# Expert units' down products: from f32 to three f16 high/low products, with the split on ScalarE and GpSimd

## What is computed

```python
def _L0_ffn_ref(hidden_states, router_w, e_bias, Wg, Wu, Wd, SWg, SWu, SWd):
    x = hidden_states.reshape(-1, orig_shape[-1])            # 2048 tokens, 128 features
    topk_idx, topk_w = _route(x, router_w, e_bias)           # 8 of 64 experts
    coef = zeros((T, E)).at[arange(T)[:, None], topk_idx].add(topk_w)
    g = einsum('th,ehi->tei', x, Wg)                         # 64 experts, 64 inner features each
    u = einsum('th,ehi->tei', x, Wu)
    h = silu(g) * u * coef[:, :, None]
    moe_out = einsum('tei,eih->th', h, Wd)
    shared = silu(x @ SWg) * (x @ SWu) @ SWd
    return (moe_out + shared).reshape(orig_shape)
```

## Time and profile before

| | |
|---|---|
| median of 3 executions | 1024.77 us (1020.2 to 1024.84) |
| span of the profiled execution | 1022.1 us (its own time isn't reported apart from the span; the span lies between the times of the three executions) |
| recurrence begins / units begin | about 43 us / 166 us |
| recurrence ends / last unit's down product | 514 us / 608 us |
| transformer block | 608 to 1022 us |
| TensorE, VectorE, GpSimd, ScalarE busy | 89%, 72%, 55%, 47% |

### The profile page before, as it was taken

How to read it: one execution, slowest core, us unless ns; L and a number is a source line. 1 busy time by engine, 2 the same in 40 slices (tenths; PEclk the granted TensorE clock), 3 DMA queues, 4 the chain that set the end, 5 groups by cost and what they waited for, 6 DMA issues and landing times. The chain is left out here.

```text
span 1022.1 us, 32080 instructions
## 1 busy us (share of the span) xinstructions
PE 910.5 (89%) x13472; PEld 719.5 (70%) x13472; DVE 737.8 (72%) x1834; ACT 479.4 (47%) x899; POOL 566.1 (55%) x516
## 2 busy tenths in 40 slices
PE   3498659999999999999998988999999999998886
PEld 3376547778777877778776866777777777777554
DVE  5766685876777676676779655878878778777655
ACT  2234323333232322223232216778787778877752
POOL 3688832343343433334354554766776766767663
PEclk9655556999999999999999997999999999999998
DMA  9212007442222222223233420000000000000001
GB/s 251 47 26 59 20 19 148 107 100 83 67 64 82 69 78 72 63 64 85 65 88 102 126 63 2 3 3 3 3 3 4 3 3 3 3 3 3 3 1 42
DMA packets 46532, 51.81 MB, mean 51 GB/s; under 512 B 22165, under 2 KB 37302, under 8 KB 46390
## 3 DMA queue, kind: packets, MB, share of 16 engines
q1 hardware_dynamic: 43472, 48.78, 18.6%
q10 hardware_dynamic: 2918, 1.01, 0.6%
HBM read 48.20 MB, written 1.57 MB: 49 GB/s over the span
## 5 line engine op out<-in xcount | busy, mean ns | idle before, releaser
L763 POOL TENSOR_TENSOR ex<-ex,xn 128x512 f32<-128x512 f32 x128 | 163.9, 1281 | 248.9 <-ACT thcb L1016 160.2
L1016 ACT ACTIVATE thcb<-ps 128x512 f32<-128x512 f32 x132 | 78.9, 598 | 205.5 <-PE ps L1874 199.5
L849 POOL TENSOR_TENSOR wu<-encC,wu 128x1024 f16<-128x1024 f32 x64 | 135.6, 2134 | 27.5 <-ACT encC L1094 27.3
L1889 PE MATMUL ps<-ex,wd 128*128 128x256 f32 x512 | 140.3, 396 | 1.3 <-POOL ex L763 0.9
L1440 DVE SCALAR_TENSOR_TENSOR ex<-thcb,ps 128x512 f32<-128x512 f32 x132 | 90.5, 686 | 50.0 <-ACT thcb L1016 45.5
L1874 PE MATMUL ps<-xnT,wg 128*128 128x256 f16 x768 | 107.1, 276 | 1.5 <-DVE ex L1446 1.4
L843 POOL TENSOR_TENSOR wd<-wd,a_sum 128x512 f32<-128x512 f32 x64 | 66.7, 1043 | 72.8 <-DVE a_sum L1571 72.6
L1874 PE MATMUL ps<-xnT,wu 128*128 128x256 f16 x768 | 106.8, 276 | 0.0
L1943 PE MATMUL ps<-wg,M 128*128 128x128 f16 x1536 | 98.5, 222 | 2.0 <-DVE wg L1540 2.0
L1943 PEld LDWEIGHTS ps<-wg,M 128*128 128x128 f16 x1536 | 93.2, 99 | 6.8 <-DVE wg L1540 2.4
L1814 PEld LDWEIGHTS ps<-eb,encC 128*128 128x128 f16 x3072 | 86.7, 98 | 14.1 <-DVE eb L1308 7.3
(11 more groups left out here) (335 smaller groups left out, 1767.5 us busy)
## 6 DMA issues: line engine op xcount, KB each, us to landing
xn<-coef_rows SPq DMA_DIRECT2D x128, 256.0 KB, 3.9
thcb<-in_L_ffn_Wg SPq DMA_DIRECT2D x8, 256.0 KB, 4.1
thcb<-in_L_ffn_Wu SPq DMA_DIRECT2D x8, 256.0 KB, 3.7
wd<-in_L_ffn_Wd SPq DMA_DIRECT2D x2, 1024.0 KB, 10.3
xtok<-in_x SPq DMA_DIRECT2D x4, 256.0 KB, 6.2
...
wu<-in_L_xcond_attn_wq SPq DMA_DIRECT2D x2, 512.0 KB, 11.1
...
```

The costliest lines, as they stand in the source:

```text
L763: nc.gpsimd.tensor_tensor(hid[:, side(m, n), :], gu[:, side(m, n), :], other, ALU.mult)\
L849: nc.gpsimd.tensor_tensor(z[:, 1, 8 * u:8 * u + 8, :], a_Zc[:, u], z[:, 0, 8 * u:8 * u + 8, :], ALU.subtract)\
L1016: nc.scalar.activation(th[:, side(m, n), :], bank(side(m, n)), ACT.Tanh, scale=0.5 / WSCALE)\
L1889: last = mm(bank(5)[:, half * HT:(half + 1) * HT], wd[:, 2 * q + p, :], hid[:, side(m, n), p * HT:(p + 1) * HT], start=(n == 0 and p == 0) ...
```

## The change

The down products become three f16 products, like the gate and up products, and 7 gaps behind the unit instead of 5. What they need is added:

- `hid` is split into two halves in `hid16` (three buffers): the high half by ScalarE at gap unit + 4, ahead of the tanh in the same gap; the low half by GpSimd at gap unit + 3 (in GpSimd's own queue, after its product of the next unit), and by VectorE at gap unit + 5, ahead of its pass, for units of odd `n` after the recurrence;
- `wd` is loaded in 8 chunks of 2 DMAs through four landing buffers and, with the shared `swd`, scaled by 16 and split in place 2 of steps 16 to 24, by ScalarE and VectorE;
- VectorE's add at a chunk's end multiplies by 1/16;
- GpSimd's product waits for both halves of the unit two before, no more for its down product; ScalarE's high half waits for the down product three units before;
- the size of the DMA scratch area is set to 1024, which makes room in SBUF.

```diff
@@ on the schedule
         def down_gap(m, n):
-            return unit_gap(m, n) + 5
+            return unit_gap(m, n) + 7
...
+        HIGH_AT = {gap + 4: u for gap, u in UNIT_AT.items()}
+        def low_by_dve(m, n):
+            return unit_gap(m, n) >= T * IDLE_GAPS and n % 2 == 1
+        LOW_POOL_AT = {gap + 3: u for gap, u in UNIT_AT.items() if not low_by_dve(*u)}
+        LOW_DVE_AT = {gap + 5: u for gap, u in UNIT_AT.items() if low_by_dve(*u)}
...
+        WD_CHUNKS = PAIRS // 4
+        WD_SPLIT = {4 * (SPC + c) + 2: c for c in range(WD_CHUNKS + 1)}
@@ SyncE
-            for a in range(2):
-                sp.dma_start(wd[a * I:(a + 1) * I, :, :],
-                             ins["L0_ffn_Wd"].rearrange("(n a) i h -> a i n h", a=2)[a]).then_inc(s["moe_w_in"], 16)
             load(SHARED + 3)
+            def load_wd(c):
+                if c >= WD_SLOTS:
+                    sp.wait_ge(s["wd_lo"], c - WD_SLOTS + 1)
+                for a in range(2):
+                    sp.dma_start(wd_land[a * I:(a + 1) * I, c % WD_SLOTS],
+                                 ins["L0_ffn_Wd"].rearrange("(n a) i h -> a i n h", a=2)[a][:, 4 * c:4 * c + 4, :])\
+                      .then_inc(s[f"wd_in{c % WD_SLOTS}"], 16)
+            for c in range(WD_SLOTS):
+                load_wd(c)
...
+                    if first(m) and half == 0 and d + WD_SLOTS < WD_CHUNKS:
+                        load_wd(d + WD_SLOTS)
@@ GpSimd
-                if others(m, n) is not None:
-                    pool.wait_ge(s["y_ready"], others(m, n))
+                if done >= 2:
+                    pool.wait_ge(s["hid_hi"], done - 1)
+                    pool.wait_ge(s[low_done(*chunk_units[done - 2])[0]], low_done(*chunk_units[done - 2])[1])
...
+            def unit_low(m, n):
+                done = m * UNITS + n
+                pool.wait_ge(s["hid_hi"], done + 1)
+                nc.gpsimd.tensor_tensor(hid16[:, done % 3, 1, :], hid[:, side(m, n), :], hid16[:, done % 3, 0, :], ALU.subtract)\
+                  .then_inc(s["hid_lo_pool"], 1)
...
                     unit(m, n)
+                if at in LOW_POOL_AT:
+                    unit_low(*LOW_POOL_AT[at])
@@ ScalarE
+            def unit_high(m, n):
+                done = m * UNITS + n
+                act.wait_ge(s["hid_ready"], done + 1)
+                if done >= 3:
+                    act.wait_ge(s["y_ready"], done - 2)
+                nc.scalar.copy(hid16[:, done % 3, 0, :], hid[:, side(m, n), :]).then_inc(s["hid_hi"], 1)
...
+                if at in WD_SPLIT:
+                    c = WD_SPLIT[at]
...
+                    wd_landed(act, c)
+                    nc.scalar.activation(wd_parts(c)[1], wd_parts(c)[0], ACT.Copy, scale=WSCALE).then_inc(s["wd_hi"], 1)
                 for what in PRO.get(at, ()):
                     part(*what)
+                if at in HIGH_AT:
+                    unit_high(*HIGH_AT[at])
                 if at in UNIT_AT:
                     unit(*UNIT_AT[at])
@@ VectorE
-                    V.tensor_tensor(dst[:, :, b], dst[:, :, b], y[:, :, b], add).then_inc(s["x2_ready"], 1)
+                    V.scalar_tensor_tensor(dst[:, :, b], y[:, :, b], 1.0 / WSCALE, dst[:, :, b], mul, add).then_inc(s["x2_ready"], 1)
...
+                if at in LOW_DVE_AT:
+                    unit_low(*LOW_DVE_AT[at])
                 if at in PASS_AT:
                     unit(*PASS_AT[at])
+                if at in WD_SPLIT:
+                    c = WD_SPLIT[at]
+                    dve.wait_ge(s["wd_hi"], c + 1)
+                    V.scalar_tensor_tensor(wd_parts(c)[2], wd_parts(c)[0], WSCALE, wd_parts(c)[1], mul, sub).then_inc(s["wd_lo"], 1)
                 if at in SPLITS:
@@ TensorE
-                pe.wait_ge(s["hid_ready"], m * UNITS + n + 1)
+                pe.wait_ge(s["hid_hi"], m * UNITS + n + 1)
+                pe.wait_ge(s[low_done(m, n)[0]], low_done(m, n)[1])
+                h16 = hid16[:, (m * UNITS + n) % 3]
...
                     for p in range(2):
-                        last = mm(bank(5)[:, half * HT:(half + 1) * HT], wd[:, 2 * q + p, :], hid[:, side(m, n), p * HT:(p + 1) * HT],
-                                  start=(n == 0 and p == 0), stop=False, skip_group_check=True)
+                        for i, (u, v) in enumerate(HALVES):
+                            last = mm(bank(5)[:, half * HT:(half + 1) * HT], wd16[:, 2 * q + p, u, :], h16[:, v, p * HT:(p + 1) * HT],
+                                      start=(n == 0 and p == 0 and i == 0), stop=False, skip_group_check=True)
```

More of the change, by code:

```diff
@@ L121, in build @@
         swd = sb("swd", [P, P])
+        wd16 = wd[:, :, :].rearrange("p n d -> p (n d)").bitcast(F16).rearrange("p (n x d) -> p n x d", x=2, d=P)
+        swd16 = sb("swd16", [P, 2, P], F16)
+        WD_SLOTS = 4
+        wd_land = sb("wd_land", [P, WD_SLOTS, 4, P])
+        hid16 = sb("hid16", [P, 3, 2, CT], F16)
         M = [sb(f"M{a}", [P, 2, H, P], F16) for a in range(2)]
@@ L338, in build @@
             "wx_hi", "wx_lo", "logits_ready", "x1_ready", "nmax_ready", "exp_ready", "en_ready", "eT_ready", "eb_hi", "eb_lo",
-            "comb_ps_ready", "comb_ready", "hn_ready", "h_ready", "rnn_dve",
+            "comb_ps_ready", "comb_ready", "hid_hi", "hid_lo_pool", "hid_lo_dve", "wd_hi", "wd_lo",
+            *(f"wd_in{i}" for i in range(4)), "swd_in", "hn_ready", "h_ready", "rnn_dve",
             "wout_ps", "flags_ready", "cnt_ready", "stats_ready", "rstd_ready", "norm_ready", "tr_ready",
```

37 lines of the change are left out of this document (29 added, 8 removed).

## The result

The changed kernel takes 1059.66 us (median of 4, 1051.57 to 1061.04), the kernel before 1022.55 (4): a ratio of 1.0331, 95% interval 1.0283 to 1.0379. The profiled execution took 1061.04 and has a span of 1059.2, 37.1 above before.

A forecast was written before the change was run, and what follows sets the result against it. TensorE was taken to bound the clean tail, a loop through tanh, VectorE and TensorE most recurrence steps. Terms 11.1 + 9.4 + 1.7 − 2.3 + 5 = +24.9 on 1024.8 gave 1050 us, range 1032 to 1064.

The forecast's parts named there:

- the ring: Clean tail: GpSimd's product, ScalarE's cast, tanh and the next product wait in a circle, 2.51 us a unit against 2.175.
- Tail: Last 20 unit intervals, no recurrence or router: 2.73 us a unit instead of 2.175, +11.1 us (+6.7 to +15.5).
- The collision: Tail: VectorE's low part and GpSimd exclude each other; GpSimd's next product loses about 0.45 us per pair of units.
- Last router stretch: 17 intervals before the clean tail: new pace plus the same 6.9 us of waits, 53.3 us, +9.4 (+2.5 to +14).
- End: After the last product: cast 0.7 and low part 1.2 before the last down product, less 0.21, +1.7 us.
- Recurrence: Steps 24 to 63, five groups of 8: gain 2.4, loss 1.95 us a group, total -2.3 (-12 to +6).
- only where VectorE isn't the bound: Recurrence: the down product before the logits gains fully in two steps of eight, about 0.14 in two: 0.7 us.
- twice that: Recurrence, upper bound: collision losses twice those forecast, giving +6 us.
- Weight splits: Steps 17 to 24: a second split per step queues behind GpSimd's product, six steps at 1 to 1.2 us; +5 (0 to +10).
- where it escapes, 0.6: Steps 17 to 24: a second weight split that avoids waiting behind GpSimd's product costs 0.6 us, otherwise up to 1.9.
- rival 4: Tail and router stretch: TensorE's clock drops to 1.2 GHz, 3.93 us a unit, 44 us more, 1094; chance 0.03.
- Signs: Tail interval 2.5 to 2.75 us, TensorE idle 0.5 to 0.8; 8 recurrence steps 58 to 59; steps 19 to 22 about 1 longer.

The follow-up runs named there:

- e4: Changed kernel with all low parts on GpSimd, none on VectorE in the tail; ratio 1.0265 to the kernel before.
- e5: Changed kernel without GpSimd's wait in the tail for the next unit's tanh; ratio 1.0231 to the kernel before.
- e7: Kernel before with only the down products made three f16 products, on other data, no high or low parts; ratio 0.9803.
- e9: Changed kernel without GpSimd's low parts before the tail, the high half read instead; ratio 1.0154 to the kernel before.
- e1: Changed kernel with ScalarE's tanh ahead of the high part after the recurrence; ratio 1.0305 to the kernel before.
- e2: Changed kernel without the weight splits of chunks 1 to 7 and the loads of chunks 4 to 7; ratio 1.0232 to the kernel before.
- e12: Changed kernel with the weight splits moved and GpSimd's pacing wait in the tail taken out; 1045.05 us, ratio 1.02 to the kernel before.
- e10: e7 with the down product seven gaps behind its unit and no GpSimd wait for it; ratio 0.9803 to the kernel before.
- e11: Changed kernel with GpSimd writing f16, two products five gaps behind, no high or low parts of the input, splits moved; 1000.71 us, ratio 0.9776.

## Why the prediction was right, and where it was off

The side, the ring and the range were right; 1059.66 lies 10 us above the forecast. By the spans it is +37.1 for +24.9: the splits, the recurrence and the rest of the kernel (+2.7, said 0) cost 15 more than said, and the tail, the router stretch and the end nearly 3 less.

- **Tail**: +9.4 for +11.1. The ring is 2.568 (e4), said 2.51: the cast to tanh 0.52 was right, the handovers were a little longer. The collision adds 0.077, not 0.22: the product behind VectorE's low part loses 0.23 (1.51 for 1.28), not 0.45, and 0.15 of that reaches a pair of units. TensorE's idle time, 0.59 a unit, is within the 0.5 to 0.8 said.
- **Last router stretch**: +8.6 for +9.4, but by another cause than stated, so the near hit is luck. The step read "17 × 2.73 + 6.9", but with the ring opened (e5) the stretch gets no shorter. VectorE is busy for 43.52 us of it, 6.6 more than in the earlier trace rows, and GpSimd for 36.65, 13.9 more; which of their waits holds it wasn't taken apart.
- **End**: the +1.7 was said of the way from the last product's end to the last down product's, and there it is +2.3. Before, 606.96 to 608.14; in the changed kernel 643.12 to 646.58:

```profile
641.84 1.28 POOL L809 TENSOR_TENSOR ex<-ex,consts 128x512 f32<-128x512 f32 x1 [0.17 <-POOL hid L815]
643.15 0.62 ACT L1078 CAST hid<-ex 128x512 f16<-128x512 f32 x1 [1.94 <-POOL ex L809]
643.85 1.15 POOL L815 TENSOR_TENSOR hid<-ex,hid 128x512 f16<-128x512 f32 x1 [0.73 <-ACT hid L1078]
645.14 1.44 PE L1972 MATMUL ps<-hid,swd 128*128 128x512 f16 x3 [1.75 <-POOL hid L815]
```

  Cast and low part cost 1.96, for 1.9 said; the down product, said to be 0.21 shorter, takes 1.44 instead of 1.12, since the granted clock is 0.50 from 643.1 on. The +1.3 of the table lie ahead of the last product's end; behind the last down product the changed kernel is 1.3 us shorter, which wasn't taken apart.
- **Recurrence**: +2.2 for -2.3. The gain was too small: "only where VectorE isn't the bound" gave 2.4 a group, but e7 gains 51.08 - 48.49 = 2.59 in seven steps and 0.60 in the eighth, 3.2 a group. The losses were right: 1.95 a group said, 50.50 - 48.49 = 2.0 measured (1.65 for the low parts by e9, 0.36 for the rest). That makes -5.8 in 39 steps (-1.19 a group of 8). What was missing are the falls of the clock, 6.0 us in steps 29, 43, 55 and 59, and the addition that changed gaps, costed at nothing: steps 35 and 51 together lose 2.3 (+4.0 and -1.7 beyond what such steps lose otherwise), a fall among it. Their sum is +2.5 against 2.2 measured. (Equal instructions took up to 2.9 us more or less in this stage, so the total proves less than the steps.) In step 45 the reciprocal comes 0.34 later than in e9, said 0.5. The upper bound of +6, "twice that", should have been +7.5 (five groups at 3.9 less 2.4).
- **Weight splits**: +12.9 in steps 18 to 23, and -0.6 in step 17, for +5 in all. This is the term that was mis-sized most; e1, with the same instructions up to there, has +8.7. Its mechanism is right (e2), and "where it escapes, 0.6" as well (the shortest new split is 0.66), but it was priced with the old split alone colliding. Both splits and GpSimd's low part collide in turn (1.47, 1.64, 1.60), so step 18 loses 2.8 at full clock where 1 to 1.2 was said. TensorE also falls to half clock for 20.5 us there. Steps 18, 20 and 22, without a fall, lose 6.8 of the 12.9 together, the three with a fall 6.1. The price of a fall can be read in step 23: 10.15 with 6.8 us at half clock, 7.34 in e1 with 0.4.
- **Clock**: rival 4 was written as all or nothing. The chip did neither; it fell in eight pieces of 3.4 or 6.8 us, 41.0 us at half clock against one piece of 3.4. In steps 24 to 62 the falls cost 8.8: the 6.0 above and 2.8 in step 35 (10.99, in e12 8.15 without a fall). The one before cost 2.2 (step 51: 10.33, in e7 8.13 without a fall). Fewer columns alone don't bring the falls: e7 and e10, with the same columns as the changed kernel, have 6.8 and 10.2 us. The four executions go the same way: the one with the higher mean clock (0.909 for 0.897) is 8 to 9.5 us shorter. That is more than the 5 us which the prediction took a measurement to tell from nothing. The Trainium skill (TensorE: Matmul & The Clock Gate, HAM oscillation — how this bites in real kernels) describes TensorE falling back after long waits, for data there. The trace agrees in so far as all five falls in steps 24 to 62 stand behind a wait, but these waits took 0.72 to 1.85 us, in a mostly busy stretch, and most waits of this length had no fall behind them.
- **Signs**: the tail's interval (2.645), the order of its waits and the longer steps 19 to 22 came as said, the steps by 1.4 to 2.7 instead of about 1. Eight steps without a fall take 50.50 + 7.03 = 57.5, just under the 58 to 59 said.

Left open: what binds the last router stretch, and what decides whether a wait of TensorE costs clock. The 1.7 us up to step 18 need no cause of their own: the experiments lie 0 to 2.5 above before there, and e1, with the same instructions as the changed kernel, 0. Why e11, with no low parts, has 27.3 us of falls wasn't taken apart either; less work on TensorE and moved splits are both in it.
